# Spreading the last batch's routing work over more steps of two expert layers, moving fill DMAs to another queue, and merging two normalizing passes

## The reference

```
x = x + linear_attention(layernorm(x))
x = x + moe(layernorm(x))            # 8 experts, top 2 of softmax gates, 128 -> 512 -> 128, relu
x = x + causal_attention(layernorm(x))
x = x + moe(layernorm(x))            # same weights
x = x + latent_and_local_attention(layernorm(x))
x = x + ffn(layernorm(x))            # 3 blocks: linear, layernorm, gelu, linear; h = y + h
x = x + mixer(layernorm(x))
x = x + ffn(layernorm(x))
```

```
shortcut = m                          # m = layernorm(x)
xn = m / (norm(m) * 128**-0.5 + 1e-8) # rms norm
u, v = silu(xn Wu + bu), silu(xn Wv + bv)
mixer = (u * causal_toeplitz_over_batches(v)) Wo + bo + shortcut
```

## Time and profile before

| | |
|---|---|
| median of 3 runs | 1555.03 us (1549.99 to 1557.27) |
| the profiled execution's own time | 1546.3 us |
| its span | 1544.5 us |
| mean granted TensorE clock in it | 0.932 |

### The profile page before, as it was taken

The page is one execution under the profiler, slowest core; times in us unless marked ns, Lnnn a source line. Parts: engine busy times, 40 slices in busy tenths (PEclk is TensorE's granted clock), DMA queues, the critical chain, the costliest instruction groups (busy, mean ns, idle before and its releaser), DMA issues. The chain is left out here.

```text
span 1544.5 us, 33714 instructions
## 1 busy us (share of the span) xinstructions
PE 1297.3 (84%) x11257; PEld 841.3 (54%) x11257; DVE 1028.3 (67%) x3074; ACT 831.6 (54%) x1425; POOL 844.0 (55%) x1254
## 2 busy tenths in 40 slices
PE   5776889887999999978899479899999987876778
PEld 4666889732344443447899234434455555644556
DVE  5765545467889988744454769887666525746976
ACT  3642123212777777742232258788555556787675
POOL 4475655434445655654554668887444305657553
PEclk9986999988999999989999579999999997988899
DMA  8012222275333333142321300000000000000001
GB/s 245 20 42 62 75 61 73 66 159 114 77 77 89 91 88 90 37 129 67 79 71 55 114 1 2 1 2 1 2 2 2 1 2 1 1 1 1 1 1 56
DMA packets 86437, 79.41 MB, mean 51 GB/s; under 512 B 11791, under 2 KB 76175, under 8 KB 85968
## 3 DMA queue, kind: packets, MB, share of 16 engines
q1 hardware_dynamic: 72434, 55.07, 14.5%
q0 software_dynamic: 8640, 17.84, 3.5%
q10 hardware_dynamic: 5196, 4.35, 1.2%
HBM read 45.94 MB, written 31.28 MB: 50 GB/s over the span
## 5 line engine op out<-in xcount | busy, mean ns | idle before, releaser
L1469 ACT ACTIVATE grp_pt<-ps 128x1024 f32<-128x1024 f32 (+2 forms) x320 | 243.8, 800 | 140.8 <-PE ps L1556 78.1
L2497 DVE TENSOR_REDUCE soft_mx<-ps 128x2 f32<-128x1024 f32 (+3 forms) x256 | 199.4, 819 | 36.2 <-PE ps L2283 35.4
L1042 POOL DMA_INDIRECT products<-moe_product,moe_rows_in x142 | 138.0, 972 | 143.8 <-DVE moe_product L1144 133.1
L2158 ACT ACTIVATE arena<-ps 128x768 f32<-128x768 f32 (+1 forms) x192 | 167.2, 881 | 81.3 <-PE ps L2316 66.6
L1061 ACT ACTIVATE moe_hid<-ps 128x512 f32<-128x512 f32 x142 | 84.3, 597 | 223.2 <-issue 107.0
L1092 PE MATMUL ps<-moe_rT,moe_W_now 128*128 128x128 f32 x1136 | 159.1, 285 | 16.5 <-DVE moe_rT L1136 8.1
L2059 POOL TENSOR_SCALAR_AFFINE_SELECT arena<-arena 128x256 f32<-128x256 f32 (+1 forms) x192 | 93.3, 488 | 122.4 <-ACT arena L2158 121.6
L1092 PEld LDWEIGHTS ps<-moe_rT,moe_W_now 128*128 128x128 f32 x1136 | 145.8, 201 | 20.4 <-DVE moe_rT L1136 13.0
L861 POOL DMA_INDIRECT sorted_rows<-route_row,route_target x128 | 127.2, 994 | 40.9 <-issue 31.2
L1571 PE MATMUL ps<-grp_pt,grp_vpad 128*32 128x160 f32 (+4 forms) x2048 | 137.6, 376 | 2.9 <-POOL grp_pt L1403 2.9
L1403 POOL TENSOR_SCALAR_AFFINE_SELECT grp_pt<-grp_pt 128x256 f32<-128x256 f32 (+1 forms) x192 | 112.1, 596 | 34.4 <-ACT grp_pt L1469 33.1
(11 more groups left out here) (375 smaller groups left out, 2852.4 us busy)
## 6 DMA issues: line engine op xcount, KB each, us to landing
moe_rows_in<-sorted_rows SPq DMA_DIRECT2D x142, 65.0 KB
route_stacks<-soft_scratch_k SPq DMA_DIRECT2D x32, 192.0 KB
arena<-products SPq DMA_DIRECT2D x8, 512.0 KB, 7.7
soft_scratch_q<-soft_parts SPq DMA_DIRECT2D x16, 192.0 KB, 2.7
route_stacks<-soft_scratch_q SPq DMA_DIRECT2D x32, 96.0 KB
arena<-products SPq DMA_DIRECT2D x4, 768.0 KB, 13.0
soft_scratch_k<-soft_parts SPq DMA_DIRECT2D x15, 192.0 KB, 2.7
products<-moe_product,moe_rows_in POOLq DMA_INDIRECT x142
```

The source lines that it names most:

```text
L1042: pool.indirect_dma_start(k.products, bass.IndirectOffsetOnAxis(rows_in[:, s % RING, DEST_COL:DEST_COL + 1].bitcast(U32), 0), product[:, s ...
L1469: act.activation(at.pair(pt[:, s % 2, :], pair, seg)[:, :, 0:w], ring[(chunks_before(m) + c) % 2][:, :, 0:w], ACT.Exp, scale=scale).then_i ...
L2158: act.activation(LATENT.pair(pt[:, s % 2, :], pair, seg)[:, :, 0:w], ring[second_turn(n, c) % RING3][:, :, 0:w], ACT.Exp, scale=scale).the ...
L2497: ins = dve.tensor_reduce(mx[:, tile, half, :, r], ring[first_turn(n, d) % RING3][:, :, at:at + keys], AX.X, ALU.max)
```

## The change

`choose` is cut in three functions with the same instructions. `rest_table` is cut in nine parts with the same instructions; only the first part and the last of them are shown. In the expert layer they are spread over steps; exponent, gates, targets and the scatters of the last batch move by two steps; `fill_end` goes from ScalarE's queue to SyncE's, behind the fetches 20 to 27. In the tail, `norm_mix` and the tile `normed` go. GpSimd computes three more 128x4 values per batch: `mix_keep` = rstd + 1, `mix_scale2` = rstd * factor, `mix_shift2` = shift * factor. `apply_mix` makes xn from x directly, with a scale and a bias. The shortcut is x * (rstd + 1) + shift, four 128x128 instructions one slot later, after `apply_mix` has read x.

```
     def choose(self, dve, m):
+        self.choose_best(dve, m)
+        self.choose_index(dve, m)
+        self.choose_hot(dve, m)
...
-    def rest_table(self, dve):
+    REST_PARTS = 9
+
+    def rest_table(self, dve, part):
...
+        if part == 0:
+            dve.wait_ge(self.steps.sem, self.steps.at(B - 1, self.PLACED))
+            dve.tensor_copy(self.fill_at[:, :], placed).then_inc(self.ends_set.sem, 1)
+            dve.tensor_scalar(self.last_edge_i[:, 0, :], placed, float(P - 1), None, ALU.add).then_inc(done, 1)
...
+        if part == 8:
+            dve.wait_ge(done, 13)
+            dve.scalar_tensor_tensor(self.tile_of[:, sure:STEPS], self.late_skip_f[:, :], self.taken_early[0:1, 0:1], self.k.steps[0:1, 0:after],
+                                     ALU.add, ALU.add).then_inc(done, 1)
+            dve.wait_ge(done, 14)
...
                 fetch(s)
+                if 20 <= s < 20 + E:
+                    route.fill_end(sp, s - 20)
...
-                if s % 3 != 1 and waiting and (waiting[0][0] < LAST or s > 8):
+                if s % 3 != 1 and waiting and (waiting[0][0] < LAST or s > 10):
                     scatter()
...
-                if s == 4:
+                if s == 6:
                     route.exponent(act, LAST)
-                if 13 <= s < 13 + E:
-                    route.fill_end(act, s - 13)
...
                     route.read_logits(dve, LAST, ps_route[1])
-                    route.choose(dve, LAST)
-                if s == 6:
+                    route.choose_best(dve, LAST)
+                if s == 4:
+                    route.choose_index(dve, LAST)
+                if s == 5:
+                    route.choose_hot(dve, LAST)
+                if s == 8:
                     route.gates(dve, LAST)
-                if s == 7:
+                if s == 9:
                     route.aim(dve, LAST, ps_route[0])
-                if s == 9:
-                    route.rest_table(dve)
+                if 11 <= s < 11 + route.REST_PARTS:
+                    route.rest_table(dve, s - 11)
...
                 pool.tensor_tensor(mix_shift[:, n % 2, :], mix_minus[:, :], mix_rstd[:, n % 2, :], ALU.mult).then_inc(mix_power.sem, 1)
+                pool.tensor_scalar(mix_keep[:, n % 2, :], mix_rstd[:, n % 2, :], 1.0, None, ALU.add).then_inc(mix_power.sem, 1)
...
+                pool.wait_ge(mix_power.sem, mix_power.at(n, 10))
+                pool.tensor_tensor(mix_scale2[:, n % 2, :], mix_rstd[:, n % 2, :], mix_factor[:, n % 2, :], ALU.mult).then_inc(mix_power.sem, 1)
+                pool.tensor_tensor(mix_shift2[:, n % 2, :], mix_shift[:, n % 2, :], mix_factor[:, n % 2, :], ALU.mult).then_inc(mix_power.sem, 1)

             def add_shortcut(n):
-                pool.wait_ge(mix_normed.sem, mix_normed.at(n))
-                x = k.x[:, n * T:(n + 1) * T, :]
-                pool.tensor_tensor(x, x, normed[:, n % 2, :, :], ALU.add).then_inc(shortcut.sem, 1)
+                pool.wait_ge(mix_normed2.sem, mix_normed2.at(n))
+                for j in range(T):
+                    x = k.x[:, n * T + j, :]
+                    ins = pool.tensor_scalar(x, x, mix_keep[:, n % 2, j:j + 1], mix_shift[:, n % 2, j:j + 1], ALU.mult, ALU.add)
+                ins.then_inc(shortcut.sem, 1)
...
-                if t - 2 in mixes:
-                    add_shortcut(mixes[t - 2])
+                if t - 3 in mixes:
+                    add_shortcut(mixes[t - 3])
...
                 for j in range(T):
-                    ins = act.activation(normed2[:, j, :], normed[:, n % 2, j, :], ACT.Copy, scale=mix_factor[:, n % 2, j:j + 1])
+                    ins = act.activation(normed2[:, j, :], k.x[:, n * T + j, :], ACT.Identity, bias=mix_shift2[:, n % 2, j:j + 1],
+                                         scale=mix_scale2[:, n % 2, j:j + 1])
...
-                if t - 1 in mixes:
-                    norm_mix(mixes[t - 1])
```

More of the change, by code:

```diff
@@ L795, in choose, with choose_index @@
         ins.then_inc(self.steps.sem, 1)
+    def choose_index(self, dve, m):
         dve.wait_ge(self.steps.sem, self.steps.at(m, self.BEST))
@@ new lines, in rest_table @@
+        if part == 0:
+            dve.wait_ge(self.steps.sem, self.steps.at(B - 1, self.PLACED))
+            dve.tensor_copy(self.fill_at[:, :], placed).then_inc(self.ends_set.sem, 1)
+            dve.tensor_scalar(self.last_edge_i[:, 0, :], placed, float(P - 1), None, ALU.add).then_inc(done, 1)
+        if part == 1:
+            dve.wait_ge(done, 1)
+            dve.tensor_scalar(self.last_edge_i[:, 1, :], self.last_edge_i[:, 0, :], 7, None, ALU.logical_shift_right).then_inc(done, 1)
+        if part == 2:
+            dve.wait_ge(done, 2)
+            dve.tensor_copy(self.last_edge[:, :], self.last_edge_i[:, 1, :]).then_inc(done, 1)
+            dve.wait_ge(done, 3)
+            dve.tensor_tensor(self.all_tiles[:, :], self.last_edge[:, :], self.k.region_tiles[0:1, :], ALU.subtract).then_inc(done, 1)
@@ new lines, in rest_table @@
+        if part == 3:
+            dve.wait_ge(done, 4)
+            dve.tensor_scalar(self.late_unused[:, :], self.all_tiles[:, :], -1.0, float(REGION_TILES), ALU.mult, ALU.add).then_inc(done, 1)
+            dve.tensor_tensor(self.late_tiles[:, :], self.all_tiles[:, :], self.taken_early[:, :], ALU.subtract).then_inc(done, 1)
+        if part == 4:
+            dve.wait_ge(done, 6)
+            dve.tensor_tensor(self.late_unused[:, 0:E - 1], self.late_unused[:, 0:E - 1], self.taken_early[:, 1:E], ALU.add).then_inc(done, 1)
+            dve.tensor_tensor(self.late_upto[:, :, :], self.late_tiles[:, :].unsqueeze(1).to_broadcast([1, E, E]), self.k.not_after[0:1, :, :],
+                              ALU.mult).then_inc(done, 1)
@@ new lines, in rest_table @@
+        if part == 5:
+            dve.wait_ge(done, 8)
+            dve.tensor_reduce(self.late_ends[:, :], self.late_upto[:, :, :], AX.X, ALU.add).then_inc(done, 1)
+            dve.wait_ge(done, 9)
+            dve.tensor_tensor(self.late_past[:, :, :], self.k.steps[0:1, 0:after].unsqueeze(2).to_broadcast([1, after, E]),
+                              self.late_ends[:, :].unsqueeze(1).to_broadcast([1, after, E]), ALU.is_ge).then_inc(done, 1)
+        if part == 6:
+            dve.wait_ge(done, 10)
+            dve.tensor_tensor(self.late_skipped[:, :, :], self.late_past[:, :, :], self.late_unused[:, :].unsqueeze(1).to_broadcast([1, after, E]),
+                              ALU.mult).then_inc(done, 1)
+            dve.tensor_reduce(self.late_expert_f[:, :], self.late_past[:, :, :], AX.X, ALU.add).then_inc(done, 1)
@@ new lines, in rest_table @@
+        if part == 7:
+            dve.wait_ge(done, 12)
+            dve.tensor_scalar(self.expert_of[:, sure:STEPS], self.late_expert_f[:, :], float(E - 1), None, ALU.min)
+            dve.tensor_reduce(self.late_skip_f[:, :], self.late_skipped[:, :, :], AX.X, ALU.add).then_inc(done, 1)
+        if part == 8:
[3 more added lines that the diff above has]
+            dve.wait_ge(done, 14)
@@ L2663, in tail @@
         mix_factor = st.sb("mix_factor", [P, 2, T], F32)
-        normed = st.sb("normed", [P, 2, T, P], F32)
+        mix_keep = st.sb("mix_keep", [P, 2, T], F32)
+        mix_scale2 = st.sb("mix_scale2", [P, 2, T], F32)
+        mix_shift2 = st.sb("mix_shift2", [P, 2, T], F32)
         normed2 = st.sb("normed2", [P, T, P], F32)
@@ L2686, in tail @@
         mix_stats_done = st.counter("mix_stats", 2)
-        mix_power = st.counter("mix_power", 9)
-        mix_normed = st.counter("mix_normed")
+        mix_power = st.counter("mix_power", 12)
         mix_normed2 = st.counter("mix_normed2")
@@ L2805, in gelu @@
                 act.activation(yT[:, i % 2, :], ps_z, ACT.Gelu, bias=k.beta[:, l:l + 1], scale=k.gamma[:, l:l + 1]).then_inc(gelu_ready.sem, 1)
-            def norm_mix(n):
-                act.wait_ge(mix_power.sem, mix_power.at(n, 4))
-                need(act, mix_normed2, mix_normed2.at(n - 2))
-                need(act, shortcut, shortcut.at(n - 2))
-                for j in range(T):
-                    ins = act.activation(normed[:, n % 2, j, :], k.x[:, n * T + j, :], ACT.Identity, bias=mix_shift[:, n % 2, j:j + 1],
-                                         scale=mix_rstd[:, n % 2, j:j + 1])
-                ins.then_inc(mix_normed.sem, 1)
             def apply_mix(n):
                 act.wait_ge(mix_power.sem, mix_power.at(n))
-                act.wait_ge(mix_normed.sem, mix_normed.at(n))
                 if n > 0:
```

45 lines of the change are left out of this document (7 added, 38 removed).

## The result

The change made the kernel faster, by less than half of what was forecast: 1547.33 us (1541.69 to 1552.44, 20 runs) against 1555.06 us (20 runs), ratio 0.9954, 95% interval 0.9942 to 0.9966. That is 7.7 us where 19 were forecast. So the traces of this first measurement can't be compared by their totals, only stage by stage.

What follows compares the result with a forecast made beforehand. No engine was full, so stages bound it: VectorE blocks and ScalarE's fills in expert layers, GpSimd and ScalarE in the tail. 2 x (3.3 + 3.8 + 2) + 1 = 19 off 1555 gives 1536 us, range 1524 to 1551.

Steps and rivals of the forecast that it cites:

- Choice in three, 3.3 us a layer: Expert layers, steps 3 to 5: splitting VectorE's 1.9 us `choose` gains 3.3 us per layer, bounds 2.3 and 4.2.
- 4.7 over: Second expert layer, steps 3 to 8: 14.22 us for 5 steps, 4.7 more than at 1.90 us each.
- a step with a piece above 2.5 us: Expert layers: the prediction is wrong if the steps with pieces stay above 2.5 us.
- Table in nine, 3.8: Expert layers, steps 11 to 19: splitting VectorE's 3.9 us `rest_table` gains 3.8 us per layer, bounds 1.9 and 5.8.
- Fills to SyncE, 2: Expert layers, steps 12 to 22: moving the fills' issue off ScalarE gains 2 us per layer of 8.1 over.
- The pairs of the earlier trace: Expert layers, steps 16 to 18: steps come in pairs of 4.9 us instead of 3.8, around ScalarE's fills.
- The rival that the pairs stay: Expert layers: slow pairs remain after the fills move, 2 x 2 us less gain, 1540 us; chance 0.20.
- SyncE's cover, nothing: Expert layers: later scatters, table and fills cost SyncE nothing; first-layer cover thin, 1 to 3 us if gone.
- Tail, -1: Tail, mixer norm in one pass: ScalarE saves 2.5 us, GpSimd adds work; net -1 us, between -4 and +8.
- above 0.7 us: Tail: the prediction is wrong if the shortcut's GpSimd instructions, taken at 0.35 us each, cost above 0.7 us.
- theory C: Follow-up theory, before near 1553 us: scatters behind sends cost 1.3 us unless VectorE blocks hide them; after's ratio 0.993 to 0.996.

Runs made afterwards that it cites:

- the run of after: Unmodified kernel after run again in a set where before took 1529.10 us: 1513.03 us, ratio 0.9884.
- the probe of ScalarE: Kernel after plus eight extra fills per routed layer, issued by ScalarE to a spare buffer in steps 44 to 58: 1518.05 us, one run.
- the spaced one: Kernel after with no scatters in two steps running and more of them ahead of the loop: 1510.99 us (0.9874); where before takes 1553 us, 1537.65 (0.9903).
- the probes: Extra scatters to a spare buffer in steps 44 to 58: on kernel after 1516.93 and 1514.78 us; on after with scatters spaced 1562.75, before 1551.11.
- the last set of runs: After, table alone, choice alone and after with scatters spaced, against before at about 1553 us: ratios 0.9943, 0.9974, 1.0012, 0.9903.

## Why the prediction was wrong

The terms were read as VectorE's and ScalarE's doing, in a profile in which part of the excess was GpSimd's scatters, which the change hardly touches. Steps are taken by the starts of `weigh`: step 4 ends with the start of `weigh` 4. At 1529 us, "with the block" is the kernel with the tail alone, and without it the run of after. Term by term:

- **Choice in three, 3.3 us a layer.** At 1529 us steps 3 to 9 take 1.7 (first layer) and 1.6 us less than with the block; step 4 was 3.2 us with it, 1.90 without (1.88 of work less 0.54 of slack is 1.3), and the clock stayed up in both (1.00 in the windows of the second layer). The run with the choice alone brought 1.0 us in both layers together, where 6.6 were forecast; its table, moved to step 11, took back 0.4 and 0.6 us in steps 9 to 14. At the first measurement's level: 16.7 before and 18.8 after in the first layer, 16.5 and 16.2 in the second. Step 4 takes 1.90 + 2 x 1.3 = 4.5 us there for the two scatters behind steps 2 and 3, and the block lay beneath. This is the step that failed: "4.7 over" was put down to the choice because it stood there. The price of 3.3 came out twice too high by the steps at one level, more than that by the run, and nothing was won at the other (the choice alone: ratio 1.0012). The sign that the prediction named for being wrong, a step with a piece above 2.5 us, came: step 4 took 4.7 us in the kernel after.
- **Table in nine, 3.8.** Mis-sized low at 1529 us: there steps 9 to 12 give 5.2 and 4.9 us a layer, and the pieces take back 0.5 and 0.9 in steps 12 to 22. The block cost twice, as predicted: its length less the slack in step 10 (5.3 to 5.5 us), then a step at a lower clock (3.8 us; the windows give 0.87 over steps 8 to 12). It has 16 instructions, not 17. At the first measurement the second layer won 5.0 us there (11.1 to 6.1), and lost 2.5 again in steps 12 to 23 (29.0 to 31.5). At that level the table alone was worth 4.8 us in both layers, not 7.6.
- **Fills to SyncE, 2.** Nothing, at 1529 us by the runs and the probe of ScalarE; at the other level not tried alone. The pairs of the earlier trace rows are scatters. The rival that the pairs stay, for which the Trainium skill was named (DMA: Bandwidth & Descriptors, Issuing engines are not separate DMA queues), was right in this point at 1529 us: moving the issue gave no time. Its time of 1540 was too low all the same, since it kept the other terms.
- **SyncE's cover, nothing.** Right for the second layer and for the fills. SyncE's waits in the kernel after, 690 to 800 us (compare; us, times, longest):

```profile
SPq L1034 <- DMA products<-moe_product,moe_rows_in: 12.7, 10, 3.1
SPq L969 <- DVE moe_fill_at L915: 1.8, 1, 1.8
```

  In the first layer there was no cover to begin with. SyncE issues the fetch of step 33 only when the last scatter has landed (it waits 20.0 us for that), and TensorE waits for its rows in step 31: 1.66 us in the kernel before, and here in the kernel after at 1529 us:

```profile
204.53 0.96 POOL L870 DMA_INDIRECT sorted_rows<-route_row,route_target  x1 [0.30 <-issue]
209.50 2.56 SPq L1035 DMA_DIRECT2D moe_rows_in<-sorted_rows  x3
211.44 0.33 PE L1105 MATMUL ps<-pack,moe_rows_in 128*128 128x128 f32 x1 [3.14 <-DMA moe_rows_in<-sorted_rows]
```

  That step takes 3.4 us before and 4.5 after in the first measurement, and 3.6 to 6.2 in all kernels at 1529 us but the spaced one, whose last scatter comes a step earlier: 1.90. This is why the spaced kernel's first layer is 3.5 us shorter than after's at 1529 us (147.1 and 150.6).

- **Tail, -1.** Right in direction, and rather too small: 1.3 us less, with an interval from 4.7 less to 0.5 more. From the first instruction on a tile of the tail to the end, the six profiles with the old tail show 267.1 to 271.2 us, the thirteen with the new one 264.7 to 267.1, on average 3.3 less. Two prices were off, both against it. Groups, the shortcut by its tile (ns: shortest, median, longest) and windows of the tail after (compare):

```profile
L2793 POOL TENSOR_SCALAR x<-x,tail_mix_keep,tail_mix_shift 128x128 f32<-128x128 f32 x32 | 20.5, 653 | 0.0
...
L2771 POOL TENSOR_SCALAR tail_mix_keep<-tail_mix_rstd 128x4 f32<-128x4 f32 x8 | 2.3, 288 | 0.0
```
```profile
L2793 POOL TENSOR_SCALAR x<-x,tail_mix_keep,tail_mix_shift x32: 445/450/2102, 1357.2 to 1459.6; 128x128 f32<-128x128 f32 x32
```
```profile
1339.00:1366.00 27.00, 19.49 (x111) 13.97 (x109) 17.05 (x88) 16.54 (x39) 22.72 (x50) 0.96 0.00 1
1366.00:1428.00 62.00, 47.38 (x222) 29.83 (x222) 43.84 (x140) 49.16 (x92) 47.40 (x88) 0.91 0.00 1
```

  The shortcut's instruction takes 0.65 us on average, not 0.35: 0.45 in 26 of the 32, and 0.85 to 2.10 in six, which all ran beside VectorE's instructions that write `tail_mixed`; only two of the 26 did. So four cost 2.6 where the one cost 1.39, and GpSimd has 2.0 us more a batch (1.2, and three small ones of 0.26 on average) instead of 0.8. It was busy 37.5 of 62 us in the stretch of ScalarE and is 47.4 now, so it has room there still. ScalarE lost 1.27 us a batch, as worked out (2.92 in two passes, 1.65 in one). The sign "above 0.7 us" for the shortcut was not met.
- **The sum.** Layers of 156.1 and 142.0 us (tail alone) became 147.2 to 150.6 and 136.2 to 136.7: with the tail 13 to 16 us, and 16 measured. At the other level 7.7 and 9.3 us were measured. The forecast of 19 is wrong at the level at which it was made. That an added scatter costs 1.3 us there and nothing at 1529 us is shown by the probes. That some of the kernel's own lay under the blocks of VectorE, and that taking the blocks away uncovered them, is read from the profiles, and theory C forecast the runs of after, table and choice by it. By the medians the level costs the kernel before 26.0 us (1529.10 to 1555.06) and after 34.3 (1513.03 to 1547.33), 8 more, and in the last set of runs 23.8 and 30.6, 7 more: five or six scatters' worth. Steps 3 to 12 of the first layer, with six scatters in either kernel, take 27.9 us in before and 25.1 at 1529 us, 2.8 for the level; in after 25.6 and 18.3, 7.3 for it. In the second layer after's profile has 14 us over that at 1529 us (150.3, 136.2) for 11 scatters in the loop, 1.3 each; before's has 10.6 over (152.6, 142.0), as if 8 of them showed. Two limits: before's profile was 9 us under its median, so its share of uncovered scatters may be read too low; and in the first layer, where the derived weights take time too, after's 19 scatters cost 12.5 us (163.1, 150.6), 0.7 each.

What sets the level is not found: GpSimd's issues, matmuls and VectorE's rows last the same at both. SyncE's rows differ. Its issues of a fetch, by tile, in the kernel after of the first measurement and of the run at 1529 us (ns: shortest, median, longest):

```profile
L1035 SPq DMA_DIRECT2D moe_rows_in<-sorted_rows x142: 3/320/712, 130.1 to 830.8; - x142
```
```profile
L1035 SPq DMA_DIRECT2D moe_rows_in<-sorted_rows x142: 337/338/727, 130.5 to 802.2; - x142
```

The shortest is 3 ns in all seven profiles at the slow level and 332 or 337 in all twelve at the other; and the time from a fetch's issue to its landing, 1.9 to 2.0 us in the median of the twelve, can be read in none of the seven, as part of the semaphore events is missing from them (13 100 to 13 500 are in each, against 17 300 to 17 700). So a profile tells its level by itself. Whether this is a cause or only goes with it, no run tells.

## What to carry to other kernels

Before a stall is put down to the work that stands in it, look at whether the engine was busy or idle in its last microsecond, and what the others issued there: here VectorE sat idle after its block until a signal came. Two causes at one place don't add, so a part's worth is known only after the other is measured alone. A mean over instructions of one shape can hide two kinds, as with the shortcut (0.45 us and 0.85 to 2.10), so the median belongs beside it. And when a rerun of the kernel before is 25 us off, compare profiles at both levels first: the difference tells what else bounds the stage.

## What the runs showed of the hardware

- Two levels of one and the same program, 1525 to 1534 and 1545 to 1560 us, constant over a set of runs and both seen on one chip. At the slow one, signals of TensorE come up to 2.8 us after the modelled end of its work while GpSimd issues two indirect DMAs 1.26 us apart, and each scatter added to a step of the second layer costs about 1.3 us (3.16 and 4.54 to 4.58 us instead of 1.90); at the other it costs nothing. One send per step leaves the step at 1.90 us at either level.
- A GpSimd memset of 128x1040 float32 (0.98 us) stretches a VectorE copy of 128x512 float32 that it meets from 0.43 to 1.93 us and costs the loop 1.2 us. In the steps of the added scatters (0.96 us each) the same copy takes 0.43 to 0.45 us in the second layer, at both levels.
- A GpSimd instruction over 128x128 with two scalar operands per partition takes 0.45 us in 26 of 32 cases, against 0.33 on average for the copy of the same shape, and 0.85 to 2.10 us in six, all beside VectorE's instructions that write `tail_mixed`.
